# A quarter of the input and seven eighths of the output by GpSimd's row-list transfers

## The reference

```python
x = L0_attn_a_u                                   # [16, 256, 128]
x = x + conv(layernorm(x))                        # long convolution by rfft/irfft, taps from exp(dt*A*t), plus u*D
x = x + ffn(layernorm(x))                         # 8 experts 128->256->128, relu, top 2 of a softmax
x = x + attn(layernorm(x))                        # 16 heads of 8, 4 query sets, causal softmax, W_proj
x = x + ffn(layernorm(x))                         # the same expert weights again
```

## Time and profile before

| | us |
|---|---|
| median of 3 runs (804.55 to 804.67) | 804.62 |
| span of the profiled execution, first to last instruction | 802.7 |
| the median less that span | 1.9 |
| PE busy in the span | 760.7 (95%) |
| ACT busy | 721.1 (90%) |
| DVE busy | 652.5 (81%) |
| POOL busy | 560.4 (70%) |

### The profile page before, as it was taken

How to read it: one execution, slowest core, us unless ns; L and a number is a source line. 1 busy time by engine, 2 the same in 40 slices (tenths; PEclk the granted TensorE clock), 3 DMA queues, 4 the chain that set the end, 5 groups by cost and what they waited for, 6 DMA issues and landing times.

```text
span 802.7 us, 20426 instructions
## 1 busy us (share of the span) xinstructions
PE 760.7 (95%) x7674; PEld 414.0 (52%) x7674; DVE 652.5 (81%) x1917; ACT 721.1 (90%) x932; POOL 560.4 (70%) x685
## 2 busy tenths in 40 slices
PE   5888999999999999999999999999989999999996
PEld 4345666677775333333333333333334777677774
DVE  7998999999876677778787777787566898989885
ACT  5918999999999999999999999999997999899984
POOL 2898665655436988888988888888896545445442
PEclk9999999999999999999999999999999999999998
DMA  9210000000044343443453334424400000000000
GB/s 276 67 64 29 1 2 2 2 2 2 8 100 106 80 93 88 98 83 90 105 107 96 90 91 90 98 67 106 107 1 2 1 15 16 15 14 16 15 15 18
DMA packets 37962, 45.70 MB, mean 57 GB/s; under 512 B 6137, under 2 KB 23810, under 8 KB 37858
## 3 DMA queue, kind: packets, MB, share of 16 engines
q1 hardware_dynamic: 37858, 44.33, 22.2%
HBM read 27.53 MB, written 16.78 MB: 55 GB/s over the span
## 4 chain that ended last, share of the span: by engine, by line
PE 54%; ACT 19%; DVE 14%; issue 11%; POOL 1%; DMA 0%; ACTq 0%; DVEq 0%; POOLq 0%
PE psum L1006 13%; ACT prob L1272 13%; PE psum L937 13%; PE psum L1316 12%; PE psum L1263 5%; DVE mixed L1025 4%; PE psum L1374 4%; ACT hidden_first L951 2%; ACT hidden_parts_first L953 2%; PE psum L1154 1%; PE psum L686 1%; DVE hidden_parts_first L960 1%; DVE hidden_parts_second L960 1%; DVE stats L362 1%; PE psum L646 1%
## 5 line engine op out<-in xcount | busy, mean ns | idle before, releaser
L1272 ACT ACTIVATE prob<-psum 128x1536 f32<-128x1536 f32 x256 | 347.6, 1499 | 14.4 <-PE psum L1263 14.4
L1279 POOL TENSOR_SCALAR_AFFINE_SELECT prob<-prob 128x512 f32<-128x512 f32 (+3 forms) x448 | 305.9, 712 | 41.1 <-ACT prob L1272 31.7
L1316 PE MATMUL psum<-prob,vstack 128*32 128x256 f32 (+1 forms) x2048 | 204.9, 495 | 1.6 <-DVE o_tok L1324 1.6
L937 PE MATMUL psum<-xt_parts,w_parts 128*128 128x512 f16 x768 | 186.6, 379 | 0.0
L1025 DVE SCALAR_TENSOR_TENSOR mixed<-psum,comb_y,mixed 128x128 f32<-128x128 f32 x512 | 143.2, 340 | 1.5 <-PE psum L1006 1.5
L967 POOL TENSOR_TENSOR hidden_parts_second<-hidden_second,hidden_parts_second 128x512 f16<-128x512 f32 x64 | 77.4, 1209 | 93.5 <-ACT hidden_parts_second L953 93.5
L967 POOL TENSOR_TENSOR hidden_parts_first<-hidden_first,hidden_parts_first 128x512 f16<-128x512 f32 x64 | 77.6, 1213 | 78.1 <-ACT hidden_parts_first L953 78.1
L1263 PE MATMUL psum<-qstack,kstack 32*128 32x512 f16 x768 | 99.7, 385 | 9.2 <-ACT prob L1272 7.8
L1263 PEld LDWEIGHTS psum<-qstack,kstack 32*128 32x128 f16 x768 | 24.9, 91 | 157.3 <-ACT prob L1272 138.7
L937 PEld LDWEIGHTS psum<-xt_parts,w_parts 128*128 128x128 f16 x768 | 71.2, 98 | 64.1 <-issue 1.4
L951 ACT ACTIVATE hidden_second<-psum,b 128x512 f32<-128x512 f32 x128 | 88.4, 691 | 15.4 <-PE psum L937 12.0
(11 more groups left out here) (148 smaller groups left out, 848.4 us busy)
## 6 DMA issues: line engine op xcount, KB each, us to landing
qstack<-qk_parts SPq DMA_DIRECT2D x128, 128.0 KB, 3.5
qk_parts<-parts SPq DMA_DIRECT2D x64, 192.0 KB, 3.1
kstack<-qk_parts SPq DMA_DIRECT2D x128, 32.0 KB, 3.5
stream<-u_folded SPq DMA_DIRECT2D x4, 512.0 KB, 8.1
kept_x<-stream SPq DMA_DIRECT2D x4, 512.0 KB, 2.6
out<-mixed SPq DMA_DIRECT2D x7, 256.0 KB, 2.3
w_whole<-L_ffn_W SPq DMA_DIRECT2D x1, 1024.0 KB, 9.0
taps<-c_taps SPq DMA_DIRECT2D x1, 640.0 KB, 7.1
```

Source lines behind the costliest of these rows:

```text
L937: last = e.matmul(bank(u % 4), m.w1[:, w_part, ex, cols], xt_parts[:, s, x_part, :], start=(n == 0), stop=(n == len(PRODUCTS) - 1))
L1272: e.activation(prob[:, n % PROBS, :], psum[:, TILE * (n % 2):TILE * (n % 2 + 1)], ACT.Exp, scale=SCALE)\
L1279: return e.affine_select(kept, kept, [[0, kept.shape[1]], [0, 2], [sign, P]], ALU.is_ge, 0.0, base=0, channel_multiplier=-sign)
L1316: last = e.matmul(to[SLOT * lane:SLOT * (lane + 1)], vstack[:, b % 2, keys, first:first + SLOT], weights_of(n - t, lane, keys, pair), star ...
```

## The change

The last quarter of the input (tiles 24 to 31) is no longer loaded by SP's fourth transfer of 512 KB. POOL issues eight indirect transfers in its place, one per tile of 128 rows of 512 bytes, each reading its row numbers from a column of a new table `row_no`, which SP loads second. They stand in POOL's queue behind the clearing of `weight` and ahead of the whole convolution. `vector_conv_stats` waits for all eight.

In the second expert block, each of the first seven chunks is stored by POOL in four such transfers (28 in all) behind the low parts of experts 3, 4, 5 and 6 of the next chunk. SP's seven transfers go; its two for the last chunk stay, and SP waits for both kinds at the end.

```diff
+        "c_rows": np.arange(TILES * P, dtype=np.uint32).reshape(TILES, P).T.copy(),
...
+    row_no = sb("row_no", [P, TILES], U32)
...
-        e.wait_ge(s_x[ch], 16)
+        e.wait_ge(s_x[ch], 16 if ch + 1 < CONV_CHUNKS else 16 * CONV_TILES)
...
         e.dma_start(tap_cols[:], dr["tap_cols"]).then_inc(s_cols, 16)
+        e.dma_start(row_no[:], dr["c_rows"]).then_inc(s_row_no, 16)
         load_x(0)
...
         e.dma_start(w2_whole[:], w2_rows).then_inc(s_w2, 16)
-        load_x(3)
...
+    def gpsimd_load_last(e):
+        e.wait_ge(s_row_no, 16)
+        for t in range((CONV_CHUNKS - 1) * CONV_TILES, CONV_CHUNKS * CONV_TILES):
+            e.indirect_dma_start(out=stream[:, t, :], out_offset=None, in_=dr["u_folded"].rearrange("b s m -> (b s) m"),
+                                 in_offset=bass.IndirectOffsetOnAxis(ap=row_no[:, t:t + 1], axis=0))\
+             .then_inc(s_x[CONV_CHUNKS - 1], 16)
...
+    def gpsimd_store_tile(e, ch, i):
+        t = ch * FFN_TILES + i
+        if i == 0:
+            e.wait_ge(accum, EXPERTS * (second.at + ch + 1))
+        e.indirect_dma_start(out=out_rows, out_offset=bass.IndirectOffsetOnAxis(ap=row_no[:, t:t + 1], axis=0),
+                             in_=mixed[:, t, :], in_offset=None).then_inc(s_rows_stored, 16)
...
                 gpsimd_low(e, second, ch, ex)
+                if ch and ex in (3, 4, 5, 6):
+                    gpsimd_store_tile(e, ch - 1, ex - 3)
...
-    STORED = 16 * (FFN_CHUNKS + 1)
+    STORED = 16 * 2
+    ROWS_STORED = 16 * (FFN_CHUNKS - 1) * FFN_TILES
...
-        for ch in range(FFN_CHUNKS - 1):
-            sync_store(e, second, ch, s_stored)
...
         e.wait_ge(s_stored, STORED)
+        e.wait_ge(s_rows_stored, ROWS_STORED)
...
         gpsimd_taps(e)
+        gpsimd_load_last(e)
         gpsimd_conv(e)
```

More of the change, by code:

```diff
@@ L274, in build_in @@
     s_x = [sem(f"landed_x{i}") for i in range(CONV_CHUNKS)]
-    s_kept, s_stored = sem("kept_x_stored"), sem("out_stored")
+    s_kept, s_stored, s_rows_stored, s_row_no = (sem(n) for n in (
+        "kept_x_stored", "out_stored", "out_rows_stored", "landed_row_no"))
     SMALL, EXPW, ATTW = 2 * 16, 6 * 16, 2 * 16
@@ L1737, in vector_second @@
             vector_accumulate(e, second, *due)
+    out_rows = out.rearrange("b s m -> (b s) m")
+    def gpsimd_store_tile(e, ch, i):
[4 more added lines that the diff above has]
+                             in_=mixed[:, t, :], in_offset=None).then_inc(s_rows_stored, 16)
     def gpsimd_second(e):
```

## The result

| | before | after |
|---|---|---|
| median, 4 executions each | 804.64 us (804.55 to 805.78) | 807.97 us (807.72 to 809.05) |
| ratio, 95% interval | | 1.0042 (1.0029 to 1.0055) |
| span of the profiled execution | 802.7 us | 806.1 us |

The account below looks back on a forecast made before the run. PE, then ACT and DVE, were taken to bound the kernel. SP 0, start 1.9 and second expert block 0 on the 802.7 us span gave 804.6, with 1.9 around it 806.5 us; range 804.3 to 813.0.

Parts of the forecast that it names:

- SP's side: SP's queue: dropping its fourth load and seven stores gains 0, and adding the row-number load costs 0.
- D: POOL's time for one indirect transfer of 128 rows, taken as 1.4 us.
- The bounds of 0.42 and 4.74: Ends for POOL's time per transfer, in us: SP's issue with a free queue, and with full transfer engines.
- the likeness to `rstd`: POOL's time per transfer: working out 128 addresses resembles `rstd` (1.05 to 1.64 us), smaller than its larger form.
- `rstd` at 14.5, ACT's spare 0.5, 1.9 us to the end: Start: eight transfers make POOL's `rstd` 2.4 us late; ACT's 0.5 spare leaves 1.9 passing down the chain.
- Loads in time: Input loads: third quarter slips 0 to about 2 us, under 3.7 to spare; fourth lands before DVE needs it; cost 0.
- Second expert block: POOL's 28 stores, 39 us of work, hide wholly beside PE's 2.64 us per expert; cost 0.
- the 1.48 allowed: Second expert block: POOL's 1.16 us plus one transfer stays under PE's pace up to 1.48 us per transfer.
- Rival 1: Start: transfers take at most 1.3 us each, cost 0 to 1.1 us; time 804.6, up to 805.7; chance 0.37.
- Rival 2: Start: DVE's first product and `grid` wait for POOL's transfers, about 4 us beside the 1.9; time 810.5; chance 0.13.
- Rival 3: Second expert block: 28 transfers slow DVE by 1.0 us each, 5 to 8 us showing; time 812; chance 0.05.
- Rival 4: PE's clock dip at 27 to 29 us disappears, winning 1.8 us if transfers also fit; time 802.8; chance 0.05.

Follow-up runs that it names:

- run 6: Kernel before with one edit: SP issues the plain load of the last quarter ahead of that of the first; 804.28 us, ratio 0.9996.
- run 7: Kernel before, with the last quarter loaded by POOL as one plain transfer behind the clearing of `weight`; 804.49 us, ratio 1.0005.
- run 9: Changed kernel with stores back on SP and POOL's eight load transfers waiting until DVE's `grid` is done; 812.07 us, ratio 1.0080.
- run 8: Changed kernel with only four of the eight load transfers on POOL, the other four tiles and all stores by SP; 804.71 us, ratio 1.0005.
- run 2: Changed kernel with the load given back to SP and only the 28 stores kept on POOL; 804.88 us, ratio 0.9997.

## Why the prediction was right, and where it was not

The side (slower, 0.52) and the range held; 806.5 was 1.5 too low. Two terms account for that: the copy's path, 1.0 us, and the stores, 0.4 us. That the side held although another path decided is partly luck: both paths are delayed by the same eight transfers.

- **SP's side, 0.** Right. Where SP issues the load, or whether it issues it at all, changes nothing (runs 6 and 7).
- **D, 1.4 us.** Right as a mean: 1.39, and by luck. The bounds of 0.42 and 4.74 were far away on both sides. The figure is a mean of two things that the likeness to `rstd` did not hold: 0.94 + 0.30 us when POOL is left alone, and up to 1.97 for some of those beside DVE's instructions with two operands in SBUF.
- **`rstd` at 14.5, ACT's spare 0.5, 1.9 us to the end.** This mechanism is real: 14.41 + 2.32 = 16.73 would be 1.95 late. Run 9 measures the spare as 0.40 (`rstd` 7.90 late, `normed` 7.50) and shows that the rest arrives whole at the end. At the top of the range the sum has a slip: 804.6 + 8.7 is 813.3, not 813.0.
- **The term that was short.** In the changed kernel this path did not decide. The step "the rest, 1.9 us, goes down the chain" took POOL's queue as the only one that the transfers delay. It took ACT's `ktap`, done at 14.76, as fixed. But `ktap` hangs on the copy of `tap_rows`, which came 2.95 late, and so `normed` was 1.0 later than the forecast. The copy's path was the one that decided already before (12.32 + 2.46 = 14.78, against 14.39 by POOL), with no spare at all. I asked what a transfer does to POOL and not what it does to the other engines' signals.
- **Loads in time, 0.** Right: DVE's statistics of the fourth quarter wait for nothing. The third quarter was nearer than reckoned: issued at 5.76 and 12.8 us on its way, it landed at 18.6 where the kernel before had it at 15.5. That is 3.1 later, more than the 0.4 + 2 reckoned at most, and under the 3.7 to spare.
- **Second expert block, 0.** Nearly: POOL keeps PE's pace, with 1.14 us a transfer against the 1.48 allowed, but the block takes 0.4 us longer in every kernel with these stores. The reckoning asked whether POOL is late on the whole and not where its passes then meet DVE's.
- **Rival 1, they fit.** Wrong with eight; right with four (run 8).
- **Rival 2, POOL and DVE take turns.** Half right, on the other engine: `grid` still takes 4.10 us, and it is POOL's transfer that stretches. The Trainium skill, "SBUF — State Buffer", section "Who interferes with whom", reports that a `tensor_tensor` of VectorE was not seen to stall a DMA, and infers the reason. For transfers with a list these runs point the other way: up to 2.01 us beside `grid`, none above 1.22 behind it (run 9). But one beside the weight product took 0.96 and one beside `grid` 1.00 us, so this is no fixed price.
- **Rival 3.** Wrong in its place and size: DVE's low parts (L970) took 0.850 us in the mean in that stretch, 0.869 before. Another pass of DVE was the slower one (run 2), and the block lost 0.4 us.
- **Rival 4, the dip goes.** It did go, and gained nothing. The clock was 1.00 from 24 to 32 us, and the eight transforms spanned 4.3 us instead of 5.37.

```profile
28.35 1.95 PE L656 MATMUL psum<-folded,forward 128*128 128x512 f32 x4 [1.77 <-POOL folded L423]
30.65 1.98 PE L656 MATMUL psum<-folded,forward 128*128 128x512 f32 x4 [0.35 <-DVE prod L666]
33.78 6.68 PE L696 MATMUL psum<-yhat,inverse 128*128 128x512 f32 x15 [1.14 <-POOL yhat L678]
```

PE then waited 1.14 us for POOL's `yhat`, and began the inverse at 33.78, 3.0 later than before.

## What to carry to other kernels

Before giving GpSimd transfers with a list, count 1.25 us of its queue for each 128 rows (of 128 to 512 bytes in these runs), add for neighbours that read two operands, and see what is queued behind: here the same load as one plain transfer cost 1.1 us and nothing in time. Then look at the second-tightest path into the same instruction, for a term that is right on one path is a lower bound only. A slack measured by one big delay (run 9) is cleaner than one read off a timeline. And where the executions scatter by 3 us, a cost of 0.4 us is found by comparing the same stretch in many traces, not by the median.

## What the runs showed of the hardware that was not expected

- A transfer with a list of 128 rows kept GpSimd for 0.94 us and the next began 0.30 us later, for rows of 128, 256 and 512 bytes alike; beside VectorE's two-operand instructions some took 1.2 to 2.0 us.
- PE's signal to another engine, due at 12.3 us, was seen 1.1 to 4.4 us late in six kernels, all with such a transfer in the making at that moment or just ended, by VectorE as by ScalarE. Other signals during such transfers were on time. The profile names the wait "remote" where it is longest, and the same six traces lack records of other semaphores.
- Twenty-eight stores of 128 rows by GpSimd's list, wholly beside TensorE's work, still cost 0.37 to 0.40 us in all seven kernels that have them.
- TensorE's granted clock fell to 0.50 near 595 us in some profiled executions and not in others, and made 2.8 us of difference; a median of few executions can hide or fake that much.
